# Surface flow on one Trainium2 core: when the units of the next group are released to TensorE

## The reference

```python
def _derivs(u):
    ux, uy = _dwconv(u, SOBEL_X), _dwconv(u, SOBEL_Y)
    uxx, uxy, uyy = _dwconv(ux, SOBEL_X), _dwconv(ux, SOBEL_Y), _dwconv(uy, SOBEL_Y)
    return clip10(ux), clip10(uy), clip10(uxx), clip10(uxy), clip10(uyy)

def step(u, _):
    ux, uy, uxx, uxy, uyy = _derivs(u)
    g2 = ux * ux + uy * uy
    K = clip5((uxx * uyy - uxy * uxy) / (max(1 + g2, EPS) ** 2 + EPS))
    H = ((1 + uy*uy) * uxx - 2 * ux*uy*uxy + (1 + ux*ux) * uyy) / (2 * sqrt(1 + g2 + EPS) ** 3 + EPS)
    u = u + DT * clip1(alpha * K + beta * clip5(H))
    return pad_edge(u[:, :, 1:-1, 1:-1]), None

u, _ = jax.lax.scan(step, x, None, length=10)
x = 0.7 * u + 0.3 * x
```

## Time and profile before

| | before |
|---|---|
| median of 3 runs | 33319.02 us (33314.83 to 33333.28) |
| profiled execution, device time | 33304.16 us |
| its span in the profile | 33302.7 us, mean granted clock of TensorE 0.93 |
| PE busy | 30263.7 us, 91% |
| DVE busy | 27134.7 us, 81% |
| ACT busy | 24424.2 us, 73% |
| POOL busy | 11786.8 us, 35% |
| DMA queue of POOL (software) | 3655.97 MB, 61.4% of 16 engines' span |
| DMA queue of SP (hardware) | 923.44 MB, 10.2% of 16 engines' span |
| surface stage, first to last matmul | 7791 to 29577 us |

### The profile page before, as it was taken

How to read it: one execution, slowest core, us unless ns; L and a number is a source line. 1 busy time by engine, 2 the same in 40 slices (tenths; PEclk the granted TensorE clock), 3 DMA queues, 4 the chain that set the end, 5 groups by cost and what they waited for, 6 DMA issues and landing times. The chain is left out here.

```text
span 33302.7 us, 708247 instructions
## 1 busy us (share of the span) xinstructions
PE 30263.7 (91%) x264406; PEld 14087.6 (42%) x264406; DVE 27134.7 (81%) x28269; ACT 24424.2 (73%) x25873; POOL 11786.8 (35%) x10892
## 2 busy tenths in 40 slices
PE   7888888889998998999899899899989989989999
PEld 5555555554443343343343333343333434433333
DVE  8888888888997998899799799799889979963102
ACT  5666666667997998899799799799889979951010
POOL 2222222223443443444344344344434434431000
PEclk7777777779999999999999999999999999999999
DMA  1111111116998999999899899899999989999757
GB/s 23 20 20 20 19 20 20 20 20 123 175 175 165 175 175 170 169 175 175 165 175 176 165 175 176 165 175 175 174 166 175 175 165 175 175 241 342 234 183 246
DMA packets 2325306, 4877.21 MB, mean 146 GB/s; under 512 B 632480, under 2 KB 764576, under 8 KB 2322464
## 3 DMA queue, kind: packets, MB, share of 16 engines
q0 software_dynamic: 1224320, 3655.97, 61.4%
q1 hardware_dynamic: 945184, 923.44, 10.2%
q10 hardware_dynamic: 154112, 270.62, 2.2%
HBM read 745.98 MB, written 497.03 MB: 37 GB/s over the span
## 5 line engine op out<-in xcount | busy, mean ns | idle before, releaser
L871 PE MATMUL surf_ps<-surf_u,surf_matf 64*64 64x512 f32 x184960 | 20187.8, 594 | 1619.2 <-ACT surf_Cc L918 555.0
L871 PEld LDWEIGHTS surf_ps<-surf_u,surf_matf 64*64 64x64 f32 x184960 | 8267.0, 134 | 13540.9 <-issue 13534.6
L975 POOL DMA_DIRECT2D surf_u<-surf_ds x4080 | 3452.9, 1154 | 3677.5 <-DVE surf_ds L1038 3295.5
L429 POOL TENSOR_TENSOR att_pr<-att_pr,att_rs 128x1024 f32<-128x1024 f32 x1024 | 2083.9, 2055 | 5660.5 <-DVE att_rs L500 5660.5
L1179 PE MATMUL conv_ps<-conv_rows,conv_w 128*96 128x512 f32 x8256 | 3555.1, 593 | 162.9 <-DVE conv_rows L1200 110.9
L1045 DVE SCALAR_TENSOR_TENSOR surf_rH<-surf_Hc,surf_dt_ab,surf_rH 128x1024 f32<-128x1024 f32 x1360 | 1747.1, 1285 | 1955.8 <-ACT surf_rH L901 1556.5
L953 POOL DMA_DIRECT2D surf_Hc<-surf_m x1360 | 1739.2, 1279 | 3668.8 <-DMA surf_Hc<-surf_Ha 3159.3
L968 POOL DMA_DIRECT2D surf_nK<-surf_B x1360 | 1327.5, 976 | 4088.6 <-ACT surf_B L930 3886.9
L926 ACT ACTIVATE surf_p2q<-surf_pq 128x2048 f32<-128x2048 f32 x1360 | 2591.8, 1906 | 133.0 <-DVE surf_pq L1010 126.8
L471 DVE SCALAR_TENSOR_TENSOR att_acc<-att_xin,att_vec,att_acc 128x512 f32<-128x512 f32 x2048 | 2464.2, 1203 | 45.4
L206 PE MATMUL att_t<-att_ident,att_pr 128*128 128x128 f32 x8192 | 1621.7, 331 | 888.7 <-ACT att_pt L329 886.2
(11 more groups left out here) (88 smaller groups left out, 47547.7 us busy)
## 6 DMA issues: line engine op xcount, KB each, us to landing
surf_p2q<-surf_p2q POOLq DMA_DIRECT2D x1360, 512.0 KB, 10.7
surf_Hc<-surf_Ha POOLq DMA_DIRECT2D x1360, 512.0 KB, 12.3
surf_nK<-surf_B POOLq DMA_DIRECT2D x1360, 512.0 KB, 11.7
surf_Hc<-surf_m POOLq DMA_DIRECT2D x1360, 512.0 KB, 9.0
surf_u<-surf_ds POOLq DMA_DIRECT2D x1360, 256.0 KB, 5.4
surf_u<-surf_ds POOLq DMA_DIRECT2D x2720, 128.0 KB, 7.8
conv_rows<-hidden SPq DMA_DIRECT2D x688, 256.0 KB, 4.0
hidden<-conv_outs ACTq DMA_DIRECT2D x688, 192.0 KB, 4.7
```

The lines of the kernel that those rows point to most:

```text
L429: pool.tensor_tensor(pr[:, rg], pr[:, rg], rs[:, rg, :].unsqueeze(2).to_broadcast([P, WC * HEADS, N]), ALU.mult).then_inc(norm_done[rg], 1)
L871: mm = pe.matmul(ps[out, t, :], matf[rows, mat, :], u[rows, k, t, off + 2:off + 2 + W], start=(i == 0), stop=(i == len(taps) - 1))
L975: pool.dma_start(u[rows, k, t, 2:W + 2].rearrange("p a w -> p (a w)"), ds[found, t, :], accum_op=ALU.add).then_inc(u_added, 16)
```

## The change

Every pair gets a release of its own. In `boundary` the rests raise `unit_ready` by 1, and each `load_pair` is followed by `landed` (as before) and now by an increment of 4, in place of 9 after the rests and 8 at the end. For the first group the same: each pair and the rests wait for their own landing and release their own units; before, pair 1 to pair 3 and the rests were issued in one go with one wait. The order of the transfers is the same, and in `boundary` so is every wait of SP. `exchange` is not touched.

```diff
--- before.py
+++ after.py
@@ -778,17 +778,18 @@
             loads_pair, rests = 4 * KT, 2 * HI
-            load_pair(0, 0)
-            landed(16 * loads_pair)
-            sp.sem_inc(unit_ready, KT)
-            for j in range(1, FIRST):
+            c = 0
+            for j in range(HI):
+                if j == FIRST:
+                    load_rests(0)
+                    c += 16 * rests
+                    landed(c)
+                    sp.sem_inc(unit_ready, 1)
                 load_pair(0, j)
-            load_rests(0)
-            for j in range(FIRST, HI):
-                load_pair(0, j)
-            n0 = 16 * (loads_pair * HI + rests)
-            sp.wait_ge(moved, n0)
-            sp.sem_inc(unit_ready, UNITS - KT)
+                c += 16 * loads_pair
+                landed(c)
+                sp.sem_inc(unit_ready, KT)
+            n0 = c
@@ -825,7 +826,7 @@
                             load_rests(g + 1)
                             c = c + 16 * rests
                             landed(c)
-                            sp.sem_inc(unit_ready, STEP_A)
+                            sp.sem_inc(unit_ready, 1)
@@ -836,8 +837,7 @@
                         load_pair(g + 1, j)
                         c = c + 16 * loads_pair
                         landed(c)
-                if load:
-                    sp.sem_inc(unit_ready, UNITS - STEP_A)
+                        sp.sem_inc(unit_ready, KT)
```

## The result

The changed kernel takes 32901.26 us (median of 4 runs, 32890.53 to 32916.91), the kernel before 33316.93 us beside it (4 runs): a ratio of 0.9875, 95% interval 0.9858 to 0.9892. That is 416 us less, 59.4 us for each of the seven changes of groups, where 327 us and 46.7 us were forecast. The range holds it, and the direction was the forecast one; the size is a quarter above the forecast.

A forecast was written before the change was run, and what follows sets the result against it. Bound at changes of groups by SP's chain sharing the DMA engines; seven changes at 46.7 us give 327 us, 33304.2 - 327 = 32977 profiled, plus 14.9 for the median: 32992 us, range 32794 to 33214 us.

The forecast's parts named there:

- What bounds a change of groups: At a change of groups, SP's serial chain of transfers sets the time, slowed by sharing the DMA engines; 146 us each.
- No stall for pair 0: First pair of a change: lands at 10369.6 as before, PE needs it at 10392.7, so PE does not stand.
- pair 1 at 114.8 us: Second pair: store and load wholly beside running units, 72.5 and 34.2 us as for pair 0; PE stands 23.6 us.
- Rests 11.6 us: Transfers behind pair 1: 11.6 us as in the trace before, landing at 10496.0, in time for unit 8.
- Pair 2 at 96.2 us: Third pair: as long as before, without its wait for `updated`; lands at 10592.2, PE stands 22.7 us.
- Pair 3 at 83.8 us: Last pair: 3.2 + 47.5 (store) + 33.1 us, starting at a restart of PE; PE stands 15.7 us.
- two bounds of 35 and 60: Pair 3's store: 35 us with 13 us in the quiet time, or 60 us as in pair 2's row; middle 47.5.
- First group and exchange: First group's loads cost and gain nothing, bounds 0 to 5 us; the exchange stays covered with some 20 us to spare.
- The slower rivals: Changes of groups: slower chain cancels the gain, 33348 us (0.08); or rests slow too, 33447 us (0.05).
- the 353 us from which they decide: Last three pairs and rests together: above 353 us the slower case at 33447 us decides; the forecast took 306.
- Trainium skill's rule of taking turns: DMA engines alternate between queues packet by packet, so SP's landings also wait for POOL's writes; spoke against the change.
- The rival of the DMA engines' work: Changes of groups: only DMA work counts, 360 us at 0.99; gain 86 us per change, 602 in all, 32717 us; 0.15.

The follow-up runs named there:

- the cut on the kernel before: The kernel before with only its 62-row stores (4 of a pair's 16) cut into 32 and 30 rows, releases as before: 32985.41 us, ratio 0.9901.
- The delayed store: Changed kernel with SP's wait ahead of pair 3's edge rows raised to the update of new unit 4: 33144.17 us, ratio 0.9946 to the kernel before.
- The kernel with both further edits: Changed kernel with 62-row stores cut into 32 and 30 rows and next edge rows issued before waiting for a load: 32616.33 us, 0.9791 of the kernel before.
- back-only kernel: The kernel before with own releases only for pair 2 and pair 3; units 0 to 8 released together, first group as before: 33097.66 us, ratio 0.9933.

## Why the prediction was right, and where it was off

- **What bounds a change of groups.** SP's chain, stretched by the shared DMA engines. Right: a longer chain alone costs (35 us per change with SP's wait moved, 38 with 31-row stores), a shorter one alone gains (43 us per change with the cut on the kernel before). The last two leave out what the cut moves at the end of the stage.
- **No stall for pair 0; pair 1 at 114.8 us and PE standing 23.6 us.** Measured 114.3 and 18.3 us. The pieces of pair 0, taken over, held within 1 us. PE reached the end of unit 3 later against the start of the chain than I had it, hence the shorter stall.
- **Rests 11.6 us.** Measured 19.7. Taken from a place where PE had long stood; here POOL's traffic had not yet ended. This is the one term of the chain that was clearly too small.
- **Pair 2 at 96.2 us, stall 22.7 us.** Measured 93.6 and 32.1 us. The 8 us of the rests are in that stall. SP's wait for `updated` vanished with the first stall, as told.
- **Pair 3 at 83.8 us, stall 15.7 us.** Measured at most 54.2, and none. This term was mis-sized: the store's 47.5 us. I had the cause right (13 quiet us behind a restart) and averaged two bounds of 35 and 60, of which both were too high: the quiet time was 18.7 us from the restart to POOL's first DMA, 15.5 of them behind the store's first issue, and the store needed 18.3. The delayed store shows the other side, 57.2 us. Lengths between exist too: at the end of the stage in the kernel before, pair 2's store took 29.2 us (29621.38 to 29650.54) as POOL's traffic ran out. That the forecast came this near is in part luck, as its errors pull both ways. Behind pair 2's release, 15.7 us were saved because the third stall is absent and 7.7 us because units 9 to 12 ran at 15.1 us in place of 17.0 (848 matmuls in 94.1 us). Lost were 5.3 us, by which the release of pair 2 came later (the rests 8.1 us more, pair 2 2.6 us less), and 5.5 us in the last four units, at 16.6 us in place of 15.26. Together that is 12.6 us, the distance from 46.7 to 59.4. The shorter stall for pair 1 has no weight in it, since the chain sets the end.
- **First group and exchange.** Nothing, as forecast (ratio 0.9998); the exchange behind the chain brought no stall.
- **The slower rivals.** Pairs 1 to 3 and the rests took 281.8 us instead of the 353 us from which they decide. Pair 1 alone came up to the full 115 us. The Trainium skill's rule of taking turns, cited there, agrees with pair 1 in direction only: taking turns with POOL's traffic, the same store still fell from 71.8 to 42.5 us when its 62-row DMAs were cut. And the stall for pair 2 made pair 3 short again.
- **The rival of the DMA engines' work.** It gave 86 us per change as a limit. The kernel with both further edits wins 97 us per change (without the 21 us at the end of the stage), so this was no limit. What was off is the ceiling: I had taken the steady share of 0.99 for it, and that kernel reads 1.01 over 450 us. With 1.01 the same sum gives 94 us. The work itself was about right: from the kernel before to this one the stretch gains 6.0 units and 94 us of DMA time (0.80 x 450 to 1.01 x 450), 15.7 us for each, where a steady unit takes 15.1.

What stays open: what the slower DMAs do to the slots of ACT and DVE was seen only as pace (17.3 us per unit in the back-only kernel), not taken apart; and the number of DMA engines per store was read where stores run alone; beside POOL's traffic it rests on the times.

## What to carry to other kernels

When a consumer waits for a batch whose parts land one after the other, release each part as it lands; read the gain from the chain of transfers, from its start to the last release that is waited for, and then subtract what the consumers lose in pace by running beside it. A serial chain that shares its DMA engines feeds back: a long stall empties the engines, and a transfer that falls into the quiet time is short. A stall that is too short does not do it: the rests took 11.6 us when PE had stood for 55 us, but 19.7 us behind a stall of 18.3 us and 27.8 us behind one of 15.9 us. Then look at the shape of the transfers: here cutting 4 of 16 stores into row counts that divide well was worth 327 us by itself (26 of them at the end of the stage), against 416 us for the releases.

## What the runs showed of the hardware

- The same 1.9 MB store takes 18.3 us in the quiet 15 us behind a restart, 57 to 73 us beside POOL's accumulating DMAs, 42.5 us beside them with its 62-row DMAs cut into 32 and 30 rows, and 101.2 us cut into 31 and 31. With nothing beside it these are 18.6, 10.7 and 26.7 us, and the last DMAs of 62 rows run at a DMA share of 0.12, those of 31 rows at 0.07.
- The DMA share of the steady steps, 0.99 at 175 GB/s, is no ceiling: with a load running it reads 1.07, at 223 GB/s. The changed kernel behind its second restart, in the columns of the earlier trace rows:

```profile
10625.00:10660.00 35.00, 35.00 (x332) 13.22 (x328) 34.55 (x39) 34.15 (x34) 15.78 (x16) 1.00 1.07 223
```
